# Centring x3 where it is scaled, group norm batch by batch, and the weights' product as a stage, in a four-block attention kernel

## The chip, the cores and the metric

One core of a Trainium2 chip runs the whole program. The metric is device time in microseconds (us), as a median of several executions; times within the kernel come from one profiled execution.

## The reference, cut to what matters

The input x is (2, 128, 16, 16) in fp32: two batches, 128 channels, 256 positions. Four blocks follow each other:

```python
# L0: group norm (32 groups of 4 channels), q, k, v, attention over 256 positions, projection, residual
xn = ((xr - mu) * rsqrt(var + 1e-6)) * gamma + beta
# L1: position attention (16-wide q and k) and channel attention, both added to x
# L2: attention with 8 heads of 16 channels on x and an embedding; output projection and residual: x3
# L3: f = (x3 - mean_c(x3)) * rsqrt(var_c(x3) + 1e-5) * norm_g
q = dwconv3x3(conv1x1(f, q_w), q_dw)          # the same for k and v
q = softmax(q, over d) * scale ; k = softmax(k, over n)
out = silu(q @ (k^T v)) ; out = chan_ln(conv1x1(out, out_w)) + x3
h = gelu(conv1x1(chan_ln(out), ff_w1)) ; result = conv1x1(chan_ln(h), ff_w2) + out
```

The change touches the group norm of L0 and the channel norm with which L3 begins.

## The kernel before, in words

Channels lie on the 128 partitions and the 256 positions on the free axis; some tiles are held with positions on partitions (names ending in T). There is no loop over tiles at run time: each engine has a list of stages, each with a batch number, written out by hand at the end of its section (GpSimd L272, ScalarE L489, VectorE L873, TensorE L1308). Engines run their lists in order and meet through semaphores, so the order of work is that of the four lists. All eight PSUM banks are shared out by hand, batch b mostly using banks 4b to 4b+3. The input and the weights come as seven transfers: x of batch 0, pack_a in two pieces, pack_b, pack_c and the taps from SyncE's queue, x of batch 1 from ScalarE's.

The start: TensorE multiplies a tile of zeros eight times (`keep_clock`, L910), then waits for the statistics of both batches. VectorE takes statistics (L539), aggregates them (L543), adds the squared mean (L547). One matmul with a group averaging matrix (L916) serves both batches; VectorE copies its result out of PSUM (L550), forms the negated square (L553) and the variance (L556); GpSimd raises it to the power -1/2 (L224); VectorE forms scale (L559) and shift (L563) and normalises x into hn0 (L568). TensorE does three more dummy products, the product of the weights wv0 and wpT0 (L920, L921), whose result VectorE evacuates to wpvT (L572), and two more dummies. Then come the stages: q (L926) and k (L930) of the normalised x, scores (L944), maxima (L589), exponentials (L298), v (L934), transposed probabilities (L973), the mix (L1001), and x1 as t times the row scale plus xb0 (L624, L627).

The L3 block folds the channel mean into the weights: GpSimd scales the 1x1 weights by norm_g into wg (L235), TensorE multiplies them by a matrix of 1/128 (`wg_mean`, L951), VectorE subtracts the result, giving wgc (`centre_wg`, L699), and GpSimd multiplies wgc by the nine taps of q into convw (L240). x3 with positions on partitions is summed in PSUM by an identity product (`x3_ident`, L1178) and the output projection (`x3_tokens`, L1185). VectorE takes its statistics (L526, L530, L533), GpSimd the inverse root (`root3`, L221), ScalarE scales each row (`f_scale`, L392) into fT, TensorE transposes it (`f_transposes`, L1192), ScalarE evacuates it (`f_evac`, L399) with two shifted copies (L402, L403). From f: q by nine products per half with convw (`conv`, L1213), k by one product (L1199) and nine VectorE steps (`k_taps`, L789 and L792), v by one product (L1222), nine ScalarE products per batch (`v_products`, L412) and eight GpSimd additions per batch (`v_sums`, L269). Behind them: transposes of v (L1228), the context product (L1241), the output products, the feed-forward part. `ff_mean_1` (L959) is a mean matmul of the feed-forward weights, between the transposes of v of batch 1 and its context product.

The group norm's middle, on VectorE and GpSimd, in the kernel's own words:

```python
nc.vector.scalar_tensor_tensor(ve0[:, :], gs0[:, :, 1], EPS_GN, nm0[:, :], ALU.add, ALU.add).then_inc(s["ve0_d"], 1)
nc.gpsimd.tensor_tensor(rstd0[:, :], ve0[:, :], mhalf[:, 0:NB], ALU.pow).then_inc(s["rstd0_d"], 1)
```

## Time and profile before

| | us |
|---|---|
| median of 3 runs | 83.71 |
| lowest and highest | 83.67, 83.97 |
| the profiled execution | 83.64 |
| its span in the profile | 81.8 |

Of the span, TensorE is busy for 71.5 us, VectorE 57.2, ScalarE 48.7, GpSimd 30.5. The weight loads of TensorE (PEld) overlap its matmuls; an fp32 matmul appears as two instructions, so counts on TensorE are twice the number in the code. Merged pieces such as "x4" are consecutive instructions of a line. "Idle before" in brackets is the time that the engine stood still before the piece, and what ended it, as far as the profile can infer it.

### The profile page before, as it was taken

What the parts mean: (1) busy time and instruction counts of PE and PEld (TensorE: products, weight loads), DVE (VectorE), ACT (ScalarE), POOL (GpSimd) and SP (SyncE); (2) the same over time, 40 slices, a digit from 0 to 9 for tenths busy, and PEclk for the clock granted to TensorE, in tenths of its full rate; (3) what the DMA queues carried; (4) which work ended last, traced back from release to release, by engine and by line L of the source; (5) the groups of instructions that cost most, each with busy time, mean ns of one, the idle gap of its engine ahead of it and who ended that gap; (6) DMA issues with size and microseconds to landing.
All of it is one profiled execution on the core that took longest, in us unless ns stands there. A gap on an engine that the chain in (4) does not pass through costs nothing.

```text
span 81.8 us, 1629 instructions
## 1 busy us (share of the span) xinstructions
PE 71.5 (87%) x563; PEld 53.7 (66%) x563; DVE 57.2 (70%) x210; ACT 48.7 (60%) x133; POOL 30.5 (37%) x62
## 2 busy tenths in 40 slices
PE   4978999999999997939898999999998579779960
PEld 1325799847888775737456656998997277646830
DVE  1357887897678649776688243699999838898540
ACT  4300487368843608395968398997998634627530
POOL 7913450005953364000000030488878712155400
PEclk9999999999999999999999999999999999999999
DMA  1999700000000000000000000000000000000003
GB/s 17 204 331 404 288 0 0 0 0 8 0 4 0 4 0 0 0 0 8 0 0 0 8 0 0 0 0 0 8 0 4 0 0 0 4 0 0 0 3 126
DMA packets 1304, 2.91 MB, mean 36 GB/s; under 512 B 144, under 2 KB 784, under 8 KB 1296
## 3 DMA queue, kind: packets, MB, share of 16 engines
q1 hardware_dynamic: 1152, 2.68, 9.8%
q10 hardware_dynamic: 144, 0.13, 0.5%
q8 instruction: 4, 0.07, 0.3%
q14 instruction: 4, 0.03, 0.1%
HBM read 2.55 MB, written 0.26 MB: 34 GB/s over the span
## 4 chain that ended last, share of the span: by engine, by line
PE 63%; DVE 17%; POOL 7%; ACT 4%; DMA 3%; issue 2%; POOLq 0%
PE bank L1213 9%; DVE nmx L748 6%; PE bank L1112 5%; PE bank L1151 4%; DMA x<-in_x 3%; POOL vacc L269 3%; POOL rs L221 3%; PE bank L1290 3%; PE bank L1138 2%; PE bank L1055 2%; PE bank L1001 2%; PE bank L973 2%; PE bank L944 2%; PE bank L1038 2%; PE bank L1124 2%
## 5 line engine op out<-in xcount | busy, mean ns | idle before, releaser
L221 POOL TENSOR_TENSOR rs<-ve,mhalf 128x2 f32<-128x2 f32 x8 | 5.6, 696 | 23.2 <-DVE ve L533 23.1
L269 POOL TENSOR_TENSOR vacc<-vacc,vprod 128x240 f32<-128x240 f32 (+1 forms) x16 | 10.8, 675 | 5.5 <-ACT vprod L412 3.8
L376 ACT ACTIVATE pT<-bank 128x512 f32<-128x512 f32 x16 | 8.5, 602 | 1.7 <-PE bank L1138 1.3
L1213 PE MATMUL bank<-convw,fsh 128*128 128x128 f32 x72 | 9.2, 275 | 0.0
L1213 PEld LDWEIGHTS bank<-convw,fsh 128*128 128x128 f32 x72 | 8.7, 193 | 0.1
L748 DVE TENSOR_REDUCE nmx<-bank 128x2 f32<-128x512 f32 x10 | 6.4, 687 | 3.2 <-PE bank L1112 3.2
L240 POOL TENSOR_TENSOR convw<-wgc,tapw 128x128 f32<-128x128 f32 x9 | 3.8, 453 | 8.0 <-DVE wgc L699 8.0
L412 ACT ACTIVATE vprod<-bank,wc 128x256 f32<-128x256 f32 x16 | 6.6, 492 | 0.0
L792 DVE SCALAR_TENSOR_TENSOR kacc<-bank,wc,kacc 128x240 f32<-128x240 f32 (+1 forms) x16 | 6.3, 447 | 0.0
L910 PE MATMUL bank<-warm 128*128 128x512 bf16 x13 | 4.8, 517 | 1.2 <-DVE warm L535 1.2
L1112 PE MATMUL bank<-km,qm 32*128 32x256 f32 x64 | 4.6, 400 | 0.0
L1151 PE MATMUL bank<-pT,v 128*32 128x256 f32 x64 | 4.3, 385 | 0.0
L1138 PE MATMUL bank<-qa,km 32*128 32x256 f32 x64 | 4.3, 381 | 0.0
L1124 PE MATMUL bank<-wa,nmx 128*128 128x128 f32 x8 | 1.7, 297 | 2.4 <-DVE nmx L742 1.7
L371 ACT ACTIVATE km<-bank,kone,kmask 128x256 f32<-128x256 f32 x4 | 2.0, 558 | 2.9 <-PE bank L1088 2.9
L476 ACT ACTIVATE excess<-bank 128x256 f32<-128x256 f32 x6 | 2.0, 380 | 2.8 <-PE bank L1112 2.8
L288 ACT ACTIVATE k<-bank,wa 128x256 f32<-128x256 f32 x2 | 0.9, 476 | 4.5 <-PE bank L930 4.5
L1112 PEld LDWEIGHTS bank<-km,qm 32*128 32x128 f32 x64 | 2.9, 184 | 0.9 <-issue 0.5
L910 PEld LDWEIGHTS bank<-warm 128*128 128x128 bf16 x13 | 1.5, 137 | 2.9 <-issue 1.7
L1138 PEld LDWEIGHTS bank<-qa,km 32*128 32x128 f32 x64 | 3.1, 185 | 0.4 <-DVE qa L756 0.2
L1124 PEld LDWEIGHTS bank<-wa,nmx 128*128 128x128 f32 x8 | 0.8, 140 | 3.7 <-DVE nmx L742 2.6
L526 DVE BATCH_NORM_STATS2 st<-bank 128x6 f32<-128x128 f32 x8 | 2.0, 290 | 1.6 <-PE bank L1185 1.6
(215 smaller groups left out, 186.9 us busy)
## 6 DMA issues: line engine op xcount, KB each, us to landing
wc<-in_pack_c SPq DMA_DIRECT2D x1, 649.0 KB, 6.7
wb<-in_pack_b SPq DMA_DIRECT2D x1, 612.0 KB, 5.6
tapw<-in_taps SPq DMA_DIRECT2D x1, 576.0 KB, 7.6
wa<-in_pack_a SPq DMA_DIRECT2D x1, 320.0 KB, 4.5
out<-y SPq DMA_DIRECT2D x2, 128.0 KB, 1.7
x<-in_x ACTq DMA_DIRECT2D x1, 128.0 KB, 2.8
x<-in_x SPq DMA_DIRECT2D x1, 128.0 KB, 2.7
wa<-in_pack_a SPq DMA_DIRECT2D x1, 72.5 KB, 2.6
```

The lines of the kernel that those rows point to most:

```text
L221: nc.gpsimd.tensor_tensor(dst, src, mhalf[:, 0:width], ALU.pow).then_inc(done, 1)
L269: nc.gpsimd.tensor_add(vacc[b][:, oy, ox], vacc[b][:, oy, ox], vprod[n - 1][b][:, iy, ix]).then_inc(s[f"vsum_d{b}"], 1)
L376: nc.scalar.activation(pT2[u % PT2_RING][:, :, :], tiles(bank[SCORE_T_BANKS[u % HG]]), ACT.Exp).then_inc(s["e2_d"], 1)
L412: nc.scalar.activation(dst, LC[b][:, 0:N].rearrange("p (h w) -> p h w", h=H), ACT.Copy, scale=tap("vdw", *CENTRE_FIRST[n])).then_inc(s[f"v ...
L748: nc.vector.tensor_reduce(nmx2[g][:, :, col:col + 1], tiles(bank[SCORE_BANKS[i]]), AX.X, ALU.max, negate=True).then_inc(s["max2_d"], 1)
L792: nc.vector.scalar_tensor_tensor(acc, k1x1[:, iy, ix], tap("kdw", dy, dx), acc, ALU.mult, ALU.add).then_inc(s["vec"], 1)
L910: nc.tensor.matmul(dst[:, :], warm[:, 0:128], warm[:, :], start=True, stop=True)
L1112: product = nc.tensor.matmul(tiles(bank[SCORE_BANKS[i]])[:, t, :], qm2[b][rows, g, t * 128:(t + 1) * 128], keys, start=True, stop=True, ti ...
L1124: last = nc.tensor.transpose(bank[SHIFT_BANK[grp]][:, t * 128:(t + 1) * 128], nmx2[grp % NG][:, t, :], ident)
L1138: product = nc.tensor.matmul(tiles(bank[SCORE_T_BANKS[i]])[:, t, :], km2[b][rows, g, t * 128:(t + 1) * 128], qa2[b][rows, g, :], start=Tru ...
L1151: last = nc.tensor.matmul(bank[MIX_BANK[grp]][QUAD * i:QUAD * (i + 1), 0:N], v2[b][:, kt, g * C + QUAD * i:g * C + QUAD * (i + 1)], pT2[(g ...
L1213: product = nc.tensor.matmul(LA[b][:, j * C:(j + 1) * C], fsh[dx][b][:, row:row + H // NT, :].rearrange("p h w -> p (h w)"), convw[:, 3 * ...
```

## The change

x3 is now centred where it is scaled: VectorE forms minus mean times inverse root (`x3_shift`, mrs3), and ScalarE's scaling takes it as a bias. The mean matmul of the 1x1 weights and its subtraction are gone, and wg stands where wgc stood. The group norm runs batch by batch: one small mean matmul for each into bank 4b, the square by ScalarE, variance by VectorE from PSUM, one root for each batch. The product of wv0 and wpT0 becomes a stage of TensorE's list (`wpv_products`, bank 6), its evacuation the first stage of VectorE's. Seven dummy products instead of eight open the program, and the last two are gone. The stage lists of all engines are in a new order, among it: both v products of L0 together, `half_masks` early, `v_product` of L1 for batch 1 where the mean matmul was, `f_transposes` of batch 0 behind the mixed transposes of batch 1, `ff_mean_1` ahead of the second batch's transposes, `root3` of batch 1 after one sum instead of three. Waits that the new order needs are added.

```diff
-pool.wait_ge(s["ve0_d"], 1)
-nc.gpsimd.tensor_tensor(rstd0[:, :], ve0[:, :], mhalf[:, 0:NB], ALU.pow).then_inc(s["rstd0_d"], 1)
+for b in range(NB):
+    pool.wait_ge(s["ve0_d"], b + 1)
+    nc.gpsimd.tensor_tensor(rstd0[:, b:b + 1], ve0[:, b:b + 1], mhalf[:, 0:1], ALU.pow).then_inc(s["rstd0_d"], 1)
...
-pool.wait_ge(s["wgc_w"], 1)
+pool.wait_ge(s["prep_w"], PREP_WG)
 pool.wait_ge(s["tap_in"], 16)
 for t in range(TAPS):
-    nc.gpsimd.tensor_tensor(convw[:, t, :], wgc[:, C:2 * C], tapw[:, t * C:(t + 1) * C], ALU.mult).then_inc(s["conv_w"], 1)
+    nc.gpsimd.tensor_tensor(convw[:, t, :], wg[:, C:2 * C], tapw[:, t * C:(t + 1) * C], ALU.mult).then_inc(s["conv_w"], 1)
...
+for stage, b in ((xb2_sum, 0), (key_steps, 0), (xb2_sum, 1), (key_steps, 1), (root3, 0), (v_sums(1, 2), 0), (root3, 1),
+    (v_sums(2, TAPS), 0), (v_sums(1, TAPS), 1), (root4, 0), (root4, 1), (root5, 0), (root5, 1), (root6, 0),
...
+for b in range(NB):
+    act.wait_ge(s["g0_p"], b + 1)
+    nc.scalar.activation(gsq0[:, b:b + 1], bank[4 * b][:, 0:1], ACT.Square).then_inc(s["gsq_d"], 1)
...
-    act.wait_ge(s["rs3_d"], b + 1)
-    for t in range(NT):
-        nc.scalar.activation(fT[b][:, t, :], tiles(LA[b], 4)[:, t, :], ACT.Copy, scale=rs3[b][:, 0, t:t + 1]).then_inc(s["fT_d"], 1)
+    act.wait_ge(s["mrs3_d"], b + 1)
+    for t in range(NT):
+        nc.scalar.activation(fT[b][:, t, :], tiles(LA[b], 4)[:, t, :], ACT.Identity, bias=mrs3[b][:, t:t + 1],
+                             scale=rs3[b][:, 0, t:t + 1]).then_inc(s["fT_d"], 1)
...
+    (head_excess(1, 2), 1), (head_excess(1, 3), 1), (head_exps(0, 0, 3), 1), (mixed_evac_of(1), 0),
+    (head_exps(0, 3, 4), 1), (head_exps(1, 0, 4), 1), (mixed_evac_of(0), 1), (x3T_evac, 0),
+    (mixed_evac_of(1), 1), (f_scale, 0), (f_evac, 0), (o2_evac, 1), (v_products(0, 2), 0), (shift_edges, 0),
+    (v_products(2, 7), 0), (f_scale, 1), (v_products(7, TAPS), 0), (x3T_evac, 1), (f_evac, 1), (shift_edges, 1),
+    (k_exp, 0), (v_products(0, 2), 1), (q_exp, 0), (v_products(2, 8), 1), (ekT_evac, 0),
+    (v_products(8, TAPS), 1), (v3_evac, 0), (qT_evac, 0), (k_exp, 1), (q_exp, 1), (ekT_evac, 1), (o3_tanh, 0),
...
-for b in range(NB):
+def group_inputs(b):
     dve.wait_ge(s[f"x{b}_in"], 16)
     nc.vector.bn_stats(st0[b][:, :], x0[b][:, :]).then_inc(s["vec"], 1)
     vec_done("st0")
-for b in range(NB):
-    dve.wait_ge(s["vec"], vec_at("st0", b + 1))
+    dve.wait_ge(s["vec"], vec_last("st0"))
     nc.vector.bn_aggr(mv0[:, b, :], st0[b][:, :]).then_inc(s["vec"], 1)
     vec_done("mv0")
-for b in range(NB):
-    dve.wait_ge(s["vec"], vec_at("mv0", b + 1))
+    dve.wait_ge(s["vec"], vec_last("mv0"))
     nc.vector.scalar_tensor_tensor(mv0[:, b, 1:2], mv0[:, b, 0:1], mv0[:, b, 0:1], mv0[:, b, 1:2],
                                    ALU.mult, ALU.add).then_inc(s["gin0_d"], 1)
-dve.wait_ge(s["g0_p"], 1)
-nc.vector.tensor_copy(gs0[:, :, :].rearrange("p b m -> p (b m)"), bank[0][:, 0:2 * NB]).then_inc(s["vec"], 1)
...
+
+def group_variance(b):
+    dve.wait_ge(s["gsq_d"], b + 1)
+    nc.vector.tensor_scalar(ve0[:, b:b + 1], bank[4 * b][:, 1:2], EPS_GN, gsq0[:, b:b + 1],
+                            ALU.add, ALU.subtract).then_inc(s["ve0_d"], 1)
+    nc.vector.tensor_scalar_mul(gm0[:, b:b + 1], bank[4 * b][:, 0:1], A("gamma")).then_inc(s["vec"], 1)
+    vec_done("gm0")
+
+def group_norm(b):
+    dve.wait_ge(s["rstd0_d"], b + 1)
+    nc.vector.tensor_scalar_mul(a0[:, b:b + 1], rstd0[:, b:b + 1], A("gamma")).then_inc(s["vec"], 1)
+    vec_done("a0")
+    dve.wait_ge(s["vec"], vec_at("gm0", b + 1))
+    nc.vector.tensor_scalar(nb0[:, b:b + 1], gm0[:, b:b + 1], rstd0[:, b:b + 1], A("beta"),
+                            ALU.mult, ALU.subtract).then_inc(s["vec"], 1)
     vec_done("nb0")
-for b in range(NB):
     dve.wait_ge(s["vec"], vec_at("nb0", b + 1))
     nc.vector.tensor_scalar(hn0[b][:, :], x0[b][:, :], a0[:, b:b + 1], nb0[:, b:b + 1],
                             ALU.mult, ALU.subtract).then_inc(s["hn0_d"], 1)
 
+for stage, b in ((group_inputs, 0), (group_inputs, 1), (group_variance, 0), (group_variance, 1),
+    (group_norm, 0), (group_norm, 1)):
+    stage(b)
+
+def wpvT_evac(b):
+    dve.wait_ge(s["wpv_p"], 1)
+    nc.vector.tensor_copy(wpvT[:, :], bank[6][:, 0:C]).then_inc(s["wpv_w"], 1)
+    nc.vector.tensor_add(bias0[:, :], bank[6][:, C:C + 1], A("bp0")).then_inc(s["wpv_w"], 1)
...
-def centre_wg(b):
-
-    dve.wait_ge(s["wgm_p"], 1)
-    nc.vector.tensor_sub(wgc[:, :], wg[:, :], bank[7][:, 0:3 * C]).then_inc(s["wgc_w"], 1)
...
+def x3_shift(b):
+    dve.wait_ge(s["rs3_d"], b + 1)
+    nc.vector.scalar_tensor_tensor(mrs3[b][:, :], mv3[b][:, 0, :, 0], -1.0, rs3[b][:, 0, :], ALU.mult, ALU.mult).then_inc(s["mrs3_d"], 1)
...
+for stage, b in ((wpvT_evac, 0), (xb0_sum, 0), (q0_evac, 0), (q0_evac, 1), (xb0_sum, 1), (max0(0), 0), (max0(1), 0),
+    (max0(0), 1), (max0(1), 1), (sums0, 0), (half_masks, 0), (p0T_evac(0), 0), (p0T_evac(0), 1), (sums0, 1),
+    (centre_outw, 0), (x1_sum, 0), (x1_sum, 1), (q1_evac, 0), (xb1_sum, 0), (xb1_sum, 1), (q1_evac, 1),
+    (max1(0), 0), (max1(1), 0), (max1(0), 1), (p1T_evac(0), 0), (max1(1), 1), (sums1, 0), (pam_sum(0), 0),
+    (pam_sum(1), 0), (sums1, 1), (p1T_evac(0), 1), (energy_min, 0), (pam_sum(0), 1), (pam_sum(1), 1),
+    (ce_scale, 0), (ceT_evac, 0), (energy_min, 1), (outw_scale, 0), (x2_sum, 0), (ce_scale, 1), (ceT_evac, 1),
     (q2_evac, 0), (x2_sum, 1), (head_maxes(0, 0, 4), 0), (q2_evac, 1), (shift_add_of(0), 0),
     (head_maxes(1, 0, 4), 0), (shift_add_of(1), 0), (head_maxes(0, 0, 4), 1), (shift_add_of(0), 1),
+    (head_maxes(1, 0, 4), 1), (o2_norm_of(0), 0), (shift_add_of(1), 1), (o2_norm_of(1), 0), (o2_evac, 0),
+    (x3_stats, 0), (x3_shift, 0), (o2_norm_of(0), 1), (o2_norm_of(1), 1), (x3_stats, 1), (k_taps(0, 3), 0),
+    (x3_shift, 1), (k_taps(3, TAPS), 0), (k_max, 0), (q_max, 0), (k_taps(0, 6), 1), (q_norm, 0),
+    (k_taps(6, TAPS), 1), (k_max, 1), (q_max, 1), (k_sums, 0), (context, 0), (q_norm, 1), (centre_ff_1, 0),
+    (silu, 0), (k_sums, 1), (context, 1), (y_stats, 0), (silu, 1), (x4_sum, 0), (y_stats, 1), (x4_stats, 0),
+    (x4_sum, 1), (centre_ff_2, 0), (x4_stats, 1), (h_stats, 0), (h_stats, 1), (y_sum, 0), (y_sum, 1)):
...
-keep_clock(8, bank[7])
-pe.wait_ge(s["gin0_d"], NB)
-pe.wait_ge(s["a_in"], 16)
-nc.tensor.matmul(bank[0][:, 0:2 * NB], A("gmean"), mv0[:, :, :].rearrange("p b m -> p (b m)"),
-                 start=True, stop=True).then_inc(s["g0_p"], 1)
+keep_clock(7, bank[7])
+for b in range(NB):
+    pe.wait_ge(s["gin0_d"], b + 1)
+    if b == 0:
+        pe.wait_ge(s["a_in"], 16)
+    nc.tensor.matmul(bank[4 * b][:, 0:2], A("gmean"), mv0[:, b, :], start=True, stop=True).then_inc(s["g0_p"], 1)
 keep_clock(3, bank[7])
-pe.wait_ge(s["a2_in"], 16)
-nc.tensor.matmul(bank[3][:, 0:C], A("wv0"), A("wpT0"), start=True, stop=True)
-nc.tensor.matmul(bank[3][:, C:C + 1], A("wpT0"), A("bv0"), start=True, stop=True).then_inc(s["wpv_p"], 1)
-keep_clock(2, bank[7])
+def wpv_products(b):
+    pe.wait_ge(s["a2_in"], 16)
+    nc.tensor.matmul(bank[6][:, 0:C], A("wv0"), A("wpT0"), start=True, stop=True)
+    nc.tensor.matmul(bank[6][:, C:C + 1], A("wpT0"), A("bv0"), start=True, stop=True).then_inc(s["wpv_p"], 1)
...
-def wg_mean(b):
-
-    pe.wait_ge(s["prep_w"], PREP_WG)
-    nc.tensor.matmul(bank[7][:, 0:3 * C], K("cmean"), wg[:, :], start=True, stop=True).then_inc(s["wgm_p"], 1)
...
-    nc.tensor.matmul(LC[b][:, 0:N], wgc[:, 2 * C:3 * C], fsh[1][b][:, 1:H + 1, :].rearrange("p h w -> p (h w)"),
+    nc.tensor.matmul(LC[b][:, 0:N], wg[:, 2 * C:3 * C], fsh[1][b][:, 1:H + 1, :].rearrange("p h w -> p (h w)"),
...
+for stage, b in ((wpv_products, 0), (k0_product, 0), (q0_product, 0), (q0_product, 1), (k0_product, 1), (scores0(0), 0),
+    (scores0(1), 0), (scores0(0), 1), (scores0(1), 1), (v0_product, 0), (v0_product, 1), (p0_transposes(0), 0),
+    (scale0, 0), (p0_transposes(0), 1), (p0_transposes(1), 0), (p0_transposes(1), 1), (mix0(0), 0), (scale0, 1),
+    (mix0(1), 0), (mix0(0), 1), (mix0(1), 1), (qk1_product, 0), (v1_product, 0), (qk1_product, 1), (scores1, 0),
+    (xb1_transposes, 0), (v1_product, 1), (scores1, 1), (xb1_transposes, 1), (p1_transposes(0), 0),
+    (p1_transposes(1), 0), (mix1(0), 0), (mix1(1), 0), (p1_transposes(0), 1), (p1_transposes(1), 1),
+    (energy, 0), (mix1(0), 1), (mix1(1), 1), (pam_transposes, 0), (ce_transpose, 0), (embedding(1), 0),
+    (energy, 1), (outw_transpose, 0), (co_product, 0), (embedding(0), 0), (pam_transposes, 1),
+    (ce_transpose, 1), (qk2, 0), (co_product, 1), (outwg_transpose, 0), (embedding(0), 1), (embedding(1), 1),
+    (of_group(group_scores, 0), 0), (v2_product, 0), (qk2, 1), (v2_product, 1),
     (of_group(max_transposes, 0), 0), (of_group(group_scores, 1), 0), (of_group(group_scores_T, 0), 0),
     (of_group(max_transposes, 1), 0), (of_group(group_scores, 0), 1), (of_group(group_scores_T, 1), 0),
     (of_group(group_mix, 0), 0), (of_group(max_transposes, 0), 1), (of_group(group_scores, 1), 1),
     (of_group(group_scores_T, 0), 1), (of_group(group_mix, 1), 0), (mixed_transposes_of(0), 0),
+    (of_group(max_transposes, 1), 1), (mixed_transposes_of(1), 0), (of_group(group_scores_T, 1), 1),
+    (o2_transposes, 0), (x3_ident, 0), (x3_tokens, 0), (of_group(group_mix, 0), 1), (of_group(group_mix, 1), 1),
+    (mixed_transposes_of(0), 1), (x3_ident, 1), (mixed_transposes_of(1), 1), (f_transposes, 0),
+    (o2_transposes, 1), (v_1x1, 0), (x3_tokens, 1), (k_1x1, 0), (conv(0, 0, TAPS), 0), (conv(1, 0, 3), 0),
+    (f_transposes, 1), (conv(1, 3, TAPS), 0), (k_1x1, 1), (v_1x1, 1), (conv(0, 0, 6), 1), (v_transposes, 0),
+    (ek_transposes, 0), (conv(0, 6, TAPS), 1), (conv(1, 0, 6), 1), (q_transposes, 0), (conv(1, 6, TAPS), 1),
+    (ctx_product, 0), (ff_mean_1, 0), (ek_transposes, 1), (o3_product, 0), (v_transposes, 1), (q_transposes, 1),
+    (ctx_product, 1), (y_products, 0), (o3_product, 1), (ff_mean_2, 0), (yg_products, 0), (y_products, 1),
+    (x4_transposes, 0), (yg_products, 1), (h_products, 0), (x4_transposes, 1), (h_products, 1),
+    (h_transposes, 0), (h_transposes, 1), (ff_product, 0), (ff_product, 1), (y_transposes, 0), (y_transposes, 1)):
```

## Rows read from the trace of the kernel before

**Rows 1.** The page, its parts 1 and 2: busy time of each engine, granted clock of TensorE.
```profile
PE 71.5 (87%) x563; PEld 53.7 (66%) x563; DVE 57.2 (70%) x210; ACT 48.7 (60%) x133; POOL 30.5 (37%) x62
...
PEclk9999999999999999999999999999999999999999
```

**Rows 2.** Chain of waits, whole span: start us, us, what held it.
```profile
5.83 0.71 POOL rstd L224
...
7.55 0.70 PE bank L926 x2
...
9.54 1.77 PE bank L944 x8
...
15.33 0.56 PE bank L1010 x2
...
18.01 0.65 PE bank L951 x2
...
21.99 0.71 PE bank L1068 x4
...
50.57 0.60 PE bank L1222 x2
...
65.20 0.64 POOL vacc L269
...
65.88 0.44 PE bank L1228 x2
66.32 0.43 PE bank L959 x2
```

**Rows 3.** Timeline of DVE, 0 to 11: start us, us, instruction, count [idle before].
```profile
3.42 0.75 DVE L539 BATCH_NORM_STATS2 st<-x 128x6 f32<-128x256 f32 x2 [2.30 <-DMA x<-in_x]
4.09 0.30 DVE L543 BATCH_NORM_AGGREGATE mv<-st 128x2 f32<-128x6 f32 x2
...
7.09 0.73 DVE L568 TENSOR_SCALAR hn<-x,a,nb 128x256 f32<-128x256 f32 x2
...
8.29 0.48 DVE L576 TENSOR_SCALAR q<-bank,wa 128x256 f32<-128x256 f32 x1 [0.21 <-PE bank L926]
...
9.58 0.48 DVE L576 TENSOR_SCALAR q<-bank,wa 128x256 f32<-128x256 f32 x1 [0.29 <-PE bank L926]
10.01 1.33 DVE L589 TENSOR_REDUCE nmax<-bank 128x1 f32<-128x256 f32 x3
```

**Rows 4.** Timeline of PE, 0 to 11.
```profile
1.17 3.38 PE L910 MATMUL bank<-warm 128*128 128x512 bf16 x8 [1.17 <-DVE warm L535]
...
4.94 0.81 PE L910 MATMUL bank<-warm 128*128 128x512 bf16 x3
6.19 0.49 PE L920 MATMUL bank<-wa 128*128 128x128 f32 x2 [0.43 <-DMA wa<-in_pack_a]
```

**Rows 5.** Timeline of ACT, 0 to 11.
```profile
3.76 0.43 ACT L284 ACTIVATE bqk<-wa 32x2 f32<-32x2 f32 x2 [1.33 <-DMA wa<-in_pack_a]
```

**Rows 6.** Timeline of DVE, 11 to 29.
```profile
14.72 0.42 DVE L627 TENSOR_TENSOR x<-t,xb 128x256 f32<-128x256 f32 x1
...
18.70 0.56 DVE L699 TENSOR_TENSOR wgc<-wg,bank 128x384 f32<-128x384 f32 x1 [0.23 <-PE bank L951]
```

**Rows 7.** Timeline of POOL, 0 to 29.
```profile
10.75 0.58 POOL L235 TENSOR_SCALAR wg<-wc,wa 128x384 f32<-128x384 f32 x1
19.34 3.76 POOL L240 TENSOR_TENSOR convw<-wgc,tapw 128x128 f32<-128x128 f32 x9 [8.00 <-DVE wgc L699]
```

**Rows 8.** Timeline of POOL, 44 to 69.
```profile
52.12 2.34 POOL L269 TENSOR_TENSOR vacc<-vacc,vprod 128x240 f32<-128x240 f32 x3 [3.32 <-ACT vprod L412]
...
61.19 4.64 POOL L269 TENSOR_TENSOR vacc<-vacc,vprod 128x240 f32<-128x240 f32 x6 [0.46 <-ACT vprod L412]
```

**Rows 9.** Timeline of ACT, 44 to 69.
```profile
59.33 1.57 ACT L412 ACTIVATE vprod<-bank,wc 128x256 f32<-128x256 f32 x4
```

**Rows 10.** Timeline of DVE, 60.7 to 61.3.
```profile
60.89 0.42 DVE L816 TENSOR_TENSOR qn<-eq,rq 128x256 f32<-128x256 f32 x1
```

More of the change, by code:

```diff
@@ L76, in build @@
         convw = sb("convw", [128, TAPS, C])
-        wg, wgc = sb("wg", [128, 3 * C]), sb("wgc", [128, 3 * C])
+        wg = sb("wg", [128, 3 * C])
         wpvT = sb("wpvT", [128, C])
@@ L97, in build @@
         mv0 = sb("mv0", [128, NB, 2])
-        gs0 = sb("gs0", [128, NB, 2])
-        nm0, ve0, rstd0, a0, nb0 = (sb(name, [128, NB]) for name in ("nm0", "ve0", "rstd0", "a0", "nb0"))
+        gsq0, gm0, ve0, rstd0, a0, nb0 = (sb(name, [128, NB]) for name in ("gsq0", "gm0", "ve0", "rstd0", "a0", "nb0"))
         hn0 = per_batch("hn0", [128, N])
@@ L283, in _ @@
             for t in range(NT):
-                nc.scalar.activation(bqk[QUAD * t:QUAD * (t + 1), :], wa[0:QUAD, at_a["bq1"][0]:at_a["bk1"][1]], ACT.Copy).then_inc(s["bqk_w"], 1)
+                nc.scalar.activation(bqk[QUAD * t:QUAD * (t + 1), :], wa[0:QUAD, at_a["bq1"][0]:at_a["bk1"][1]], ACT.Copy)
+            for b in range(NB):
+                act.wait_ge(s["g0_p"], b + 1)
+                nc.scalar.activation(gsq0[:, b:b + 1], bank[4 * b][:, 0:1], ACT.Square).then_inc(s["gsq_d"], 1)
             def k0_evac(b):
@@ L565, in _ @@
+            def group_norm(b):
[5 more added lines that the diff above has]
+                                        ALU.mult, ALU.subtract).then_inc(s["vec"], 1)
                 vec_done("nb0")
-            for b in range(NB):
@@ L932, in v0_product @@
             def v0_product(b):
+                if b == 0:
+                    pe.wait_ge(s["wpv_w"], 1)
                 for t in range(NT):
@@ L1060, in pam_transposes @@
             def pam_transposes(b):
+                pe.wait_ge(s[f"pamT_d{NT - 1}"], b + 1)
                 for t in range(NT):
@@ L1090, in v2_product @@
             def v2_product(b):
+                pe.wait_ge((s["q2_d"], s["k2_d"])[b], NG)
                 for t in range(NT):
@@ L1176, in x3_ident @@
                     pe.wait_ge(s["e2_d"], 3 * HG + 2)
+                pe.wait_ge(s["xb2_d"], b + 1)
                 for t in range(NT):
@@ L1198, in k_1x1 @@
                 pe.wait_ge(s["f_d"], b + 1)
-                nc.tensor.matmul(LD[b][:, 0:N], wgc[:, 0:C], fsh[1][b][:, 1:H + 1, :].rearrange("p h w -> p (h w)"),
+                nc.tensor.matmul(LD[b][:, 0:N], wg[:, 0:C], fsh[1][b][:, 1:H + 1, :].rearrange("p h w -> p (h w)"),
                                  start=True, stop=True).then_inc(s["k1x1_p"], 1)
```

75 lines of the change are left out of this document (8 added, 67 removed).

## Prediction

> **What bounds the kernel now.** I read the page first: TensorE is busy for 87% of the span, no other engine for more than 70%, and the granted clock is at its top in every slice [rows 1]. So most of the span is a queue of matmuls, and work taken off the other engines is worth nothing where that queue is full. Next the chain of waits, for the places where it leaves TensorE [rows 2]. There are three that this change touches. The group norm: VectorE, one matmul and GpSimd's power alternate until the first product starts at 7.55. The middle, from the query product at 15.33 to the group scores, where the chain lies on TensorE alone, so that a matmul there costs its full length. And the depthwise sums of v: GpSimd's additions for the second batch end at 65.84, and only then come the transposes at 65.88. Last, the timelines, for what can be packed closer.
>
> Profiled execution and runs: the sum is made against the profiled execution's own 83.64 us (span 81.8), 0.07 below the median of 83.71. A difference of under 0.5%, 0.42 us, can't be told from none.
>
> **Term A, group norm per batch.** Before, statistics, aggregates and squares of both batches are ready by about 4.65 and one root serves both. Now VectorE finishes batch 0 alone: half of the 0.75 of statistics, one aggregate (some 0.15) and one square (some 0.17) with 0.04 between dependent steps bring it from 3.42 to about 4.2, and batch 1 to about 5.0 [rows 3]. That part loses 0.35, since each batch waits out its own dependent steps. The mean matmul (0.4) and the new square on ScalarE, which no row shows, fit under batch 1's statistics: a tiny activation took about 0.22 (two in 0.43) [rows 5], so batch 0's is done at about 4.85. Its bounds are 0.2 and 0.5; at the upper end the variance is 0.1 late. What goes is the copy out of PSUM and the negated square. The variance of batch 0 starts at 5.02, and the root, a tiny step and a handshake of 0.16 later, at 5.34 where it starts at 5.83 now; it takes 0.71 for two columns [rows 2]; for one column I take the same (bounds 0.5 and 0.71, the row being of the same operation). It ends at 6.05, not 6.54. Then scale, shift (one, not two) and normalisation: the normalised x begins at 6.51, and the first product at 6.9 against 7.55. Batch 1's root queues behind the first: 6.15 to 6.85, its normalised x from 7.27 to 7.62, where it ended at 7.82 [rows 3].
>
> The weights' product needs the second piece of pack_a, for which TensorE waited until 6.19 [rows 4]; it runs 6.19 to about 6.8 and hides. Its evacuation (some 0.35) and one addition of xb0 (some 0.3) now stand on VectorE before q's evacuation. That costs: q0 of batch 0 is evacuated at 8.3, no earlier than now at 8.29 [rows 3]. Yet k and q of both batches are all out of TensorE at 6.9 + 4 x 0.43 = 8.6, not at 9.54, so the scores start at 8.78 instead of 9.54 [rows 2]: 0.76. VectorE has 10.01 - 7.82 = 2.19 between normalised x and the first maximum, 0.50 of it waits for TensorE (0.21 and 0.29) [rows 3]; without them the maxima start at 7.62 + 1.69 = 9.3 at the earliest, 9.4 with the handshakes: 0.6. From there the same 4.0 us of matmuls leads to the query product, now at 15.33 [rows 2]. The half masks now stand inside this stretch (about 0.4 on VectorE, before a transposed probability tile that TensorE wants at 12.55 and gets at 12.2), so they are covered. **A = 0.70**, between 0.6 and 0.76.
>
> **Term B, no centring of the 1x1 weights.** It takes away a matmul of 0.65 on the chain at 18.01 [rows 2] and VectorE's subtraction of 0.56 at 18.70 [rows 6]. The v product of batch 1, about 0.44, moves into the same place, so the scores behind it gain only 0.2 at once. VectorE reaches the next maximum 0.6 earlier, and the first mix waits for its evacuated tile, then for nothing: following maxima, exponentials and evacuations one by one, TensorE is idle about 0.25, and the energy product at 21.99 [rows 2] comes at 20.8, that is 1.2 earlier including A. **B = 0.50**; bounds 0.2 (only the immediate gain) and 0.65 (the whole matmul). From there to 44 the order of a few stages changes; TensorE stays full to the group scores, then VectorE's maxima set the pace as now: I count nothing.
>
> GpSimd's nine tap products (3.76) waited until 19.34 for the centred weights; now they wait only for the scaled ones, ready at 11.33 [rows 7]. Nobody needs them before the convolution, which stands behind the v product at 50.57, so the gain is nothing; what they may collide with is below.
>
> **Term C, x3 centred where it is scaled.** Per batch VectorE gets one tiny product (some 0.17 like the other tiny ones, plus two hops of 0.04), and ScalarE's scaling takes a bias too, at most 0.05 more per tile. On batch 0 it is hidden: in the new order ScalarE takes the second mixed tile of batch 1 ahead of the scaling, and by my walk is busy with it until 0.4 after the shift. If that cover were gone it would cost 0.25. ScalarE now does three exponentials ahead of the mixed tile instead of one, which frees the transposed scores by about 0.6; but TensorE then takes transposes ahead of x3's. Walking all four engines through this stretch with the durations of before, the v product, now at 50.57 and 0.60 long [rows 2], ends at 51.3 against 51.17. GpSimd's sums, which start behind it at 52.12 [rows 8], start at 52.2; the second batch's root, now after one sum, waits about 0.1 for its variance. **C = -0.15**, bounds +0.3 and -0.7. From 52.12 to 65.84 these sums and the root, 16 and 1, are the bound.
>
> **Term D, behind the sums.** The feed-forward mean matmul, 0.43 between the transposes of v and the context product [rows 2], moves into TensorE's idle time. ScalarE's evacuation of v still takes 0.4 after the transposes, so 0.2 is left of it: **D = 0.20**, bounds 0 and 0.43. The x4 transposes go ahead of a product but the second batch sets the end.
>
> Sum: 0.70 + 0.50 - 0.15 + 0.20 = 1.25.
>
> **A collision, term E.** GpSimd's addition at 61.19 came 0.46 after the one before [rows 8], though its tile, the first of the four written from 59.33 on, had been ready for over a microsecond [rows 9]; just then VectorE ran a product of two SBUF operands, 60.89 to 61.23 [rows 10]. So such pairs can exclude each other. In the new order the tap products, 11.4 to 15.2, lie over VectorE's addition of t and xb0, two SBUF operands, 0.42 [rows 6], on the path at about 14.1 and again at 15.0. Each may wait for a running tap product of 0.42: from nothing to 0.42 on the first, little on the second, which has 0.15 of slack. I take 0.15. The Trainium skill (SBUF — State Buffer, "Who interferes with whom") says VectorE and GpSimd share one port pair as an exclusive lock, for two SBUF inputs and also for VectorE's fast scaling in SBUF. By that rule, the trace at 61.19 agrees; the normalised x, at 6.51, would also stand behind the second root. What it gives is a rival below.
>
> Forecast: 83.64 - 1.25 + 0.15 = 82.54, and 0.07 for the median: **82.6**. Its own range is 82.2 to 83.0.
>
> **Rivals.**
> (1) The lock in full, 0.16. Normalised x of batch 0 waits for the root of batch 1, 6.51 to 6.85, 0.35 that VectorE passes on to everything behind it, and the addition waits 0.42 more. For: the 0.46 at 61.19. Against: small VectorE steps ran beside GpSimd's roots unhindered in the tail. Result 83.64 - 1.25 + 0.77 = 83.2, with the median 83.2 to 83.3.
> (2) The order loses the gain in the conv part, 0.17: C at its bound or a little past it, since x3's scaling stands behind another evacuation on ScalarE and v's sums start 0.7 later. For: the start of the sums hangs there on a chain through all four engines, each in a new order. Against: the walk finds other work for TensorE at every point but two, 0.2 each. Result 83.64 - 1.10 + 0.6 = 83.1 to 83.5.
> (3) Slower, 0.07: TensorE's clock. The first eight dummy matmuls took 0.42 each, the three from 4.94 on 0.27 with their latency [rows 4]: same shape, so the clock went from 1.2 to 2.4 GHz at about 4.5. The change issues seven, and leaves TensorE with a tiny matmul only between 4.1 and 5.05. If the clock were still low when k's product starts, the 3.5 us of products and scores from 6.9 to 10.5 would take up to 7.0: 82.5 + 3.5 = 86.0. It decides at 6.9: rising by then it costs nothing, at 8.6 it costs 1.7, that is 84.3. Against: the granted clock is full in every slice [rows 1], and one dummy of eight is little.
> That the square could need a table of its own is the remaining mishap; it would show as a second table load before 5.
>
> **Chances.** Forecast 0.60, lock 0.16, order 0.17, clock 0.07. Faster by over 0.5% (below 83.29): nearly all of the first, three quarters of the second, half of the third: 0.58 + 0.12 + 0.08 = 0.78. Slower (above 84.13): the clock and a tail of the order: 0.08. Same: 0.14. The range 81.9 to 83.5 takes in A, B and D at their upper bounds (0.4 more) with no collision, and both middle rivals, and leaves out the clock and the tails.
>
> **What would show it.** Right: first product on hn at about 6.9, query product at 14.6, energy at 20.8, v's sums starting 1.1 to 1.2 earlier (about 51.0), transposes of v at 64.7, no wgc. Tap products right behind wg. Wrong: normalised x starting only when the second root ends; an addition at 14 that begins late; dummy products of 0.42 past 5; sums that start less than 0.8 earlier, which would put the loss in term C; or a GpSimd chain that got longer between its ends.

## The result and the profile after

The changed kernel is slower: 85.16 us as the median of four runs, against 83.76 for four runs of the kernel before beside them, a ratio of 1.0159 (95% interval 1.0133 to 1.0186). The prediction was 82.6, at most 83.5. The profiled execution took 85.18 with a span of 83.4; the one before took 83.64 with 81.8. The difference of these two, 1.54, is what is traced below. Executions of one and the same kernel fall into two groups here, around 83.8 and around 85.1, and a ratio compares the lower group where a kernel has one; the four of the changed kernel have none (85.06, 85.14, 85.18, and 86.77), the four beside them have only that.

The stages, from the chains of waits of four executions (us from the span's start; the last two columns are experiments that come below):

| start of | before | after | eighth dummy back (e1) | dense, late taps (f3) |
|---|---|---|---|---|
| scores, L0 | 9.54 | 10.56 | 9.13 | 8.85 |
| query product, L1 | 15.33 | 16.60 | 15.08 | 14.78 |
| energy product | 21.99 | 22.96 | 21.58 | 21.37 |
| first transposed maxima, L2 | 32.29 | 33.25 | 31.87 | 31.50 |
| last transposed scores, L2 | 45.27 | 45.53 | 44.15 | 43.79 |
| x3 with positions on partitions, batch 0 | 46.34 | 47.56 | 46.18 | 45.82 |
| v product, batch 0 | 50.57 | 52.24 | 50.85 | 50.50 |
| transposes of v, batch 1 | 65.88 | 67.45 | 66.06 | 65.69 |

Two things stand in it. The changed kernel is 1.02 behind before its first scores. And from the last transposed scores to the v product it loses 1.41 more, having gained 0.76 up to there.

**The page**, parts 1 and 2. Where [rows 1] stood, nothing looks wrong:

```profile
PE 73.1 (88%) x560; PEld 55.1 (66%) x560; DVE 58.3 (70%) x213; ACT 49.2 (59%) x135; POOL 31.3 (38%) x63
...
PEclk9999999999999999999999999999999999999999
```

TensorE has three instructions fewer and is busy for 1.6 us more. The same work took longer. The timeline of TensorE, 0 to 12, says where:

```profile
1.17 3.17 PE L915 MATMUL bank<-warm 128*128 128x512 bf16 x7 [1.17 <-DVE warm L540]
4.44 0.59 PE L923 MATMUL bank<-mv,wa 128*128 128x2 f32 x2
5.25 0.59 PE L923 MATMUL bank<-mv,wa 128*128 128x2 f32 x2 [0.22 <-DVE mv L550]
5.69 1.44 PE L915 MATMUL bank<-warm 128*128 128x512 bf16 x3
...
7.64 1.20 PE L936 MATMUL bank<-hn,wa 128*128 128x256 f32 x2
8.63 1.49 PE L932 MATMUL bank<-hn,wa 128*128 128x256 f32 x4
9.96 0.59 PE L936 MATMUL bank<-hn,wa 128*128 128x256 f32 x2
```

Three dummies take 1.44 where they took 0.81 [rows 4], and the first product 1.20 where it took 0.70 [rows 2]. Those are durations of the lower level, 1.2 GHz; k of batch 1, at 9.96, is the first piece wholly at the upper one, 2.4 GHz. Before, the level had risen by the dummies at 4.94. The row of the granted clock is all nines in both kernels, so it doesn't tell of this opening; the duration of a known shape does.

**VectorE, 4 to 18:**

```profile
6.08 0.22 DVE L555 TENSOR_SCALAR ve<-bank,gsq 128x1 f32<-128x1 f32 x1 [0.46 <-ACT gsq L288]
...
6.76 0.41 DVE L569 TENSOR_SCALAR hn<-x,a,nb 128x256 f32<-128x256 f32 x1
...
15.29 0.78 DVE L691 TENSOR_SCALAR outwc<-outwc,outws 128x128 f32<-128x128 f32 x1
15.49 0.57 DVE L631 TENSOR_TENSOR t<-bank,rb 128x256 f32<-128x256 f32 x1
16.12 0.42 DVE L634 TENSOR_TENSOR x<-t,xb 128x256 f32<-128x256 f32 x1
```

The variance of batch 1 stands in VectorE's list ahead of the scale of batch 0 and waits for ScalarE's square. The scaling of outwc at 15.29 takes 0.78, beside the last of GpSimd's tap products (11.71 to 15.49) and the clearing of a tile behind them (to 15.99); with the tap products moved away (f3) it takes 0.29. It also takes 0.29 in e1, where they run as here, so what is held up changes with where the steps fall. The sum x of t and xb comes late behind it, and the query product at 16.60 waits 0.28 for it.

**The chain of waits**, whole span, to set against [rows 2]:

```profile
10.56 1.77 PE bank L952 x8
...
32.09 1.03 ACT km L375 x2
...
45.53 1.15 PE bank L1141 x16
46.68 0.38 PE bank L1173 x2
47.06 0.02 issue
47.08 0.44 DVE o L774
47.52 0.04 issue
47.56 0.71 PE bank L1189 x4
48.27 1.86 PE bank L1154 x32
50.14 0.37 PE bank L1166 x2
50.51 0.45 PE bank L1182 x4
50.95 0.23 PE bank L1166 x2
...
51.80 0.44 PE bank L1173 x2
52.24 0.60 PE bank L1226 x2
...
66.62 0.79 POOL vacc L269
67.40 0.04 issue
67.45 0.45 PE bank L1232 x2
67.92 0.39 ACT v L437
68.31 0.04 issue
68.36 0.71 PE bank L1245 x4
```

The transposed scores of the last group run ahead of three pieces that ran before them in the old order: the transposes of o2 (L1173), VectorE's copy of them, and x3's identity product. Then come the 32 matmuls of the mix and the second mix's transposes. From 51.18 to 51.80 TensorE has only the transposes of f to do and waits for VectorE, before the last transposes of o2, which now stand ahead of the v product. That is 2.03 to x3 and 4.68 on to the v product, where it was 1.07 and 4.23. A second chain ends nearly as late there: ScalarE's scaling of x3 and the evacuation of f, which the v product reads, end at 52.08 (the line at 51.70 below).

**Shift and scaling of x3**, both batches, VectorE and then ScalarE, 47 to 60:

```profile
50.14 0.16 DVE L781 SCALAR_TENSOR_TENSOR mrs<-mv,rs 128x2 f32<-128x2 f32 x1 [0.84 <-POOL rs L220]
...
55.56 0.41 DVE L781 SCALAR_TENSOR_TENSOR mrs<-mv,rs 128x2 f32<-128x2 f32 x1
```

```profile
50.49 0.80 ACT L396 ACTIVATE fT<-bank,mrs,rs 128x128 f32<-128x128 f32 x2
51.70 0.39 ACT L404 ACTIVATE fsh<-bank 128x256 f32<-128x256 f32 x1 [0.42 <-PE bank L1196]
...
56.00 0.81 ACT L396 ACTIVATE fT<-bank,mrs,rs 128x128 f32<-128x128 f32 x2
```

The shift (mrs) takes 0.16 with GpSimd quiet and 0.41 while GpSimd adds products of v. Scaling with a bias takes 0.80 for two tiles; without one it took 0.62 (g4 below).

### The profile page after: what moved, and what is told of

The parts are those of the page before. It is cut to its first block, busy times and chain, and to the rows that moved or that the text cites. A ratio compares the mean times of both kernels' runs of the same rounds, so it can differ in the third digit from the quotient of the medians.

```text
span 83.4 us, 1630 instructions
## 1 busy us (share of the span) xinstructions
PE 73.1 (88%) x560; PEld 55.1 (66%) x560; DVE 58.3 (70%) x213; ACT 49.2 (59%) x135; POOL 31.3 (38%) x63
## 4 chain that ended last, share of the span: by engine, by line
PE 57%; DVE 16%; ACT 11%; POOL 7%; DMA 3%; issue 3%; POOLq 0%
PE bank L1115 5%; PE bank L1217 5%; POOL vacc L269 4%; ACT vprod L417 4%; DMA x<-in_x 3%; DVE nmx L750 3%; POOL rs L220 3%; PE bank L1294 2%; ACT pT L380 2%; PE bank L1056 2%; PE bank L1141 2%; PE bank L1154 2%; PE bank L1090 2%; PE bank L952 2%; PE bank L1039 2%
## 5 line engine op out<-in xcount | busy, mean ns | idle before, releaser
L246 POOL TENSOR_SCALAR xb<-x,wa 128x256 f32<-128x256 f32 x2 | 2.3, 1147 | 11.0 <-DVE x L722 11.0
L240 POOL TENSOR_TENSOR convw<-wg,tapw 128x128 f32<-128x128 f32 x9 | 3.8, 457 | 0.1
```

Of the source, the lines that this page charges most:

```text
L240: nc.gpsimd.tensor_tensor(convw[:, t, :], wg[:, C:2 * C], tapw[:, t * C:(t + 1) * C], ALU.mult).then_inc(s["conv_w"], 1)
```

## Experiments

Theory T: the clock of the opening makes the time, because seven dummies stand where eight stood. Rivals: the added waits and orders, the two engines' collision, the centring itself.

**e1, the eighth dummy back, and nothing else.**

```diff
-            keep_clock(7, bank[7])
+            keep_clock(8, bank[7])
```

> The changed kernel with eight opening dummy products instead of seven. Clock theory: the array was still at the low level up to 9.6 in the changed kernel because TensorE did too little before 4.6; with the eighth the products of k and q run at the high level, the scores start at about 9.0 to 9.2 and not 10.56, and the time is 83.6 to 83.9, 1.3 to 1.5 below the changed kernel. Rival (the gap between the two mean matmuls keeps the clock low, whatever the eighth does): scores at 10.5, time 85.1.

Ten executions: five at 83.72 to 83.86, five at 85.05 to 85.74; ratio of the lower group 0.9997 (0.9978 to 1.0016). The profiled one took 83.79. TensorE, 0 to 11:

```profile
5.57 0.81 PE L915 MATMUL bank<-warm 128*128 128x512 bf16 x3
...
7.13 0.70 PE L936 MATMUL bank<-hn,wa 128*128 128x256 f32 x2 [0.42 <-DVE hn L569]
```

Every stage of the table is 1.38 to 1.52 earlier than in the changed kernel: a rise of the clock ahead of the first products instead of at about 9.6 is worth 1.4. It makes up all but 0.15 of the difference of 1.54.

That the eighth dummy brings the early rise is not shown. Five of ten executions with it are still in the upper group, and against four of four without it that can be chance (probability 0.13 if both had one rate). What is shown is that this loss belongs to the changed opening. The mean granted clock tells the two losses apart: with the late rise it reads 1.00 (the changed kernel's profile), with a fall at 66 it reads 0.98 (e2 below). All 32 upper executions of the kernel before with its eight dummies, of 81 in three series, read 0.975 to 0.980. Of the 28 of the changed kernel, e1, e3 and e4 together, 14 are in the upper group with 1.00.

**e2, the kernel before with seven dummies.** The same edit on the other side (8 to 7).

> The kernel before with seven opening dummy products instead of eight, nothing else. Clock theory with the count as its cause: the clock stays low here too, the scores start 1 to 2 late and the time is 84.8 to 85.8. Rival (the spread of the small products is the cause): unchanged, 83.7.

All four executions at 85.09 to 85.14, ratio 1.0157 (1.0137 to 1.0177), next to the changed kernel's 1.0159. Its start, however, is at the upper level: the three dummies at 4.99 take 0.81. The clock falls late; page, then TensorE's timeline, 60 to 74:

```profile
PEclk9999999999999999999999999999999858999999
```

```profile
65.92 0.69 PE L1228 MATMUL bank<-wa,vacc 128*128 128x128 f32 x2 [1.16 <-POOL vacc L269]
66.40 1.06 PE L959 MATMUL bank<-w1g,wc 128*128 128x256 f32 x2
...
67.68 1.06 PE L1241 MATMUL bank<-v,ekT 128*128 128x128 f32 x4
```

L959 takes 1.06 where it took 0.60, behind an idle wait of 1.16 for GpSimd's last sum that the kernel before has too. So there are two places where the level can be lost, the opening and the wait at 65, and either costs 1.3 to 1.5. The mean clock of this execution is 0.977. Two of the changed kernel's own runs show 0.976 (85.06) and 0.98 (86.77), so it loses in either place, the second perhaps in both. What ties the number of dummies to a fall at 66 no run shows: the kernel before falls there with eight as well, in 32 of 81 executions. At that rate four of four in the upper group would be chance once in 40, so seven may make it likelier. One of the four (85.09) reads 1.00 and was not profiled; it may have lost at the opening.

**e3, a dummy between the two mean matmuls of the changed kernel** (seven opening ones kept), and **e4, eight dummies and the tap products held back until x1 is summed:**

```diff
 nc.tensor.matmul(bank[4 * b][:, 0:2], A("gmean"), mv0[:, b, :], ...)
+if b == 0:
+    keep_clock(1, bank[7])
```
```diff
 pool.wait_ge(s["tap_in"], 16)
+pool.wait_ge(s["x1_d"], NB)
```

> The changed kernel with one dummy product between the two mean matmuls, seven ahead as it has them. If the idle time between 4.1 and 5.25 is what holds the clock down, this brings the scores to 9.0 to 9.3 and the time to 83.7 to 84.0; if only what TensorE did before about 4.5 counts, the scores stay at 10.5 and the time at 85.1 or a little above, since the dummy delays the second mean by up to 0.2.

> Eight opening dummies as in the first run, and GpSimd's tap products wait until both x1 are there (about 15.5) instead of starting right behind the scaled weights. Lock theory: VectorE's scalings and its addition into x1 no longer meet them, the query product comes 0.2 earlier than in the first run, and the time is 0.1 to 0.25 lower (the opposite risk: they now meet VectorE's work from 16 to 20). Rival: no difference, within 0.1.

e3: five of ten at 83.58 to 83.93, five at 84.86 to 85.87; with the gap filled or with a dummy ahead, half of the executions lose. e4: one of four at 83.55, the rest at 84.90 to 85.35, and in its profile, eight dummies or not, the three behind the mean matmuls take 1.44. Its time says nothing of the taps. Its profile, with a late rise as in the changed kernel's, has 5.79 from the scores to the query product against 6.04, but 12.38 against 12.40 to the energy product: the tap products then meet VectorE's next work. Nothing of the size of a few tenths can be read while the clock is left to chance, so the next kernels fill both places.

**f1, the kernel before with its late waits filled:** two dummies ahead of the transposes of k's exponentials of batch 1, four ahead of those of v of batch 1.

```diff
+def fill(n):
+    return lambda b: keep_clock(n, bank[4])
-(ctx_product, 0), (ek_transposes, 1), (o3_product, 0), (v_transposes, 1)
+(ctx_product, 0), (fill(2), 1), (ek_transposes, 1), (o3_product, 0), (fill(4), 1), (v_transposes, 1)
```

> The kernel before with six dummy products in TensorE's idle time behind the context product of batch 0 (two, then four, ahead of the transposes of v of batch 1). Theory: the executions at 84.9 to 85.1 that the kernel before also has lose their time to the clock, which falls once in that idle stretch (between 63 and 66) and is low for some 3 us; with TensorE kept busy there, that loss goes and executions lie at 83.6 to 84.0, but for those where the clock rises late at the start. Rival (the falls come from elsewhere): the two levels remain as often as in the kernel before, which has 7 of 19 at the upper one.

All ten executions at 83.41 to 83.92, median 83.77, ratio 1.000 (0.998 to 1.002), while 11 of the 31 unfilled ones beside them took 84.91 or more. The other versions of the kernel before with this filling (g1, g2, g4) don't fall into two groups either. TensorE, 60 to 70: the wait of 1.16 is down to 0.29, and L959 takes its 0.60.

```profile
64.86 1.03 PE L910 MATMUL bank<-warm 128*128 128x512 bf16 x4
66.19 0.44 PE L1231 MATMUL bank<-wa,vacc 128*128 128x128 f32 x2 [0.29 <-POOL vacc L269]
66.47 0.60 PE L959 MATMUL bank<-w1g,wc 128*128 128x256 f32 x2
```

**f2, the changed kernel made dense:** e1 and e3 together, one dummy behind the weights' product, and four ahead of the transposes of v of batch 1. **f3** is f2 with e4's wait; **f4** is f2 with the stage lists of all engines, from 43 to 53, in the order of before:

```diff
-(mixed_evac_of(0), 1), (x3T_evac, 0), (mixed_evac_of(1), 1), (f_scale, 0), (f_evac, 0), (o2_evac, 1)
+(mixed_evac_of(0), 1), (f_scale, 0), (mixed_evac_of(1), 1), (f_evac, 0), (x3T_evac, 0), (shift_edges, 0)
...
-(root3, 0), (v_sums(1, 2), 0), (root3, 1), (v_sums(2, TAPS), 0)
+(root3, 0), (v_sums(1, 4), 0), (root3, 1), (v_sums(4, TAPS), 0)
```

> The changed kernel with eight opening dummies, one between the two mean matmuls, one behind the weights' product, and four in the idle time ahead of the transposes of v of batch 1. Theory: what the change costs is the clock alone and, with that mended, its orders give 83.7 to 83.9, no better than the kernel before. The profile should show the high level before 8 and no fall later; the upper level (85) should be gone or rare. Rival (dummies don't help the start): still 85 in half of the executions.

> As the filled changed kernel, with GpSimd's tap products held until both x1 are written. Lock theory: the additions into x1 and the scalings take their usual 0.20 to 0.43 instead of up to 0.57, the query product comes 0.1 to 0.2 earlier against the filled changed kernel, and the time is 0.1 to 0.2 lower, unless the tap products meet other steps of VectorE later. Rival: within 0.1.

> As the filled changed kernel, with the stage order between the last transposed scores and the convolution (TensorE, ScalarE, VectorE, and the second root of GpSimd) put back to that of the kernel before; centring by the bias stays. Theory that the new order there costs 0.7: the v product comes 0.6 to 0.8 earlier and the time is 83.1 to 83.3 against 83.8. Rival (centring by a bias costs the 0.7 itself, through the extra step and the longer scaling): it stays within 0.2 of the filled changed kernel.

| kernel | median of 10 | lowest to highest | ratio (95%) |
|---|---|---|---|
| f1, before, filled | 83.77 | 83.41 to 83.92 | 1.000 (0.998 to 1.002) |
| f2, after, dense | 83.94 | 83.70 to 84.24 | 1.0027 (1.0004 to 1.0049) |
| f3, f2 with late taps | 83.63 | 83.42 to 83.95 | 0.9967 (0.993 to 1.0005) |
| f4, f2 with the old order | 84.99 | 84.68 to 85.45 | 1.0154 (1.0128 to 1.018) |

None of these four kernels falls into two groups. f2 against the changed kernel: 1.2, the clock's; which of its dummies does it is not separated. f2 against f1: with the clock held, the change is worth 0.17 in the wrong direction, which is no difference by the measure of 0.42. f3 against f2: 0.31, though its profile shows only 0.11 of it between the scores and the query product (5.93 against 6.04 from one to the other), and that is lost again by the energy product (12.52 against 12.40 from the scores); its x also arrived 0.08 earlier. Where the 0.31 lie stays open. Its VectorE, 11 to 18, with nothing held up until the tap products start at 15.80; then xb takes 0.98 where it took 0.62:

```profile
13.46 0.29 DVE L692 TENSOR_SCALAR outwc<-outwc,outws 128x128 f32<-128x128 f32 x1
13.85 0.42 DVE L632 TENSOR_TENSOR t<-bank,rb 128x256 f32<-128x256 f32 x1
14.30 0.42 DVE L635 TENSOR_TENSOR x<-t,xb 128x256 f32<-128x256 f32 x1
...
16.30 0.98 DVE L648 TENSOR_SCALAR xb<-x,gbv 128x256 f32<-128x256 f32 x2
```

f4 says that the new order, blamed above for 1.41 on the way to the v product, is a repair: without it the centring costs 1.05 more. The v product of batch 0 was expected 0.6 to 0.8 earlier and comes at 50.62 against 50.67 in f2: with the order of the exponentials put back as well, the last transposed scores start at 45.18 against 44.05. And batch 1 pays. VectorE and ScalarE of f4, 53 to 59:

```profile
55.47 0.56 DVE L781 SCALAR_TENSOR_TENSOR mrs<-mv,rs 128x2 f32<-128x2 f32 x1
```

```profile
56.06 0.81 ACT L396 ACTIVATE fT<-bank,mrs,rs 128x128 f32<-128x128 f32 x2 [1.77 <-DVE mrs L781]
```

The root now stands behind three sums, the shift behind the root and beside a fourth sum, and ScalarE stands still for 1.77 in front of its scaling, with the products of v for GpSimd queued behind it.

**g1, the centring alone, in the kernel before** (filled as f1): wg for wgc, no mean matmul, shift and bias as in the change, everything else and its order as before, the taps held back to x1. **g4** is g1 without shift and bias: it leaves out the centring of x3. **g2** is f1 with the group norm per batch alone, and e3's dummy. **g3** is f3 with x3 centred and scaled by VectorE in one step for each tile instead of the shift and ScalarE's scaling:

```diff
-nc.vector.scalar_tensor_tensor(mrs3[b][:, :], mv3[b][:, 0, :, 0], -1.0, rs3[b][:, 0, :], ALU.mult, ALU.mult)
+for t in range(NT):
+    nc.vector.tensor_scalar(fT[b][:, t, :], tiles(LA[b], 4)[:, t, :], mv3[b][:, 0, t, 0:1], rs3[b][:, 0, t:t + 1], ALU.subtract, ALU.mult)
```

> The kernel before with the filled idle time, and of the change only x3 centred by the bias (no mean matmul, no subtraction, one shift step per batch, tap products behind x1); group norm and all orders as before. Theory: the mean matmul gives back 0.4, but the shift and the longer scaling lengthen the chain from x3 to the v product by 0.45 for batch 0 and, behind root and tap steps, more for batch 1, so the time is 83.8 to 84.6 against 83.78 of the filled kernel before. Rival (the bias is free, as forecast): 83.2 to 83.4.

> As the centring-only kernel but with no shift either: x3's mean is not subtracted at all, so this leaves out the centring of the channel norm (the output is not the reference's). Only the mean matmul and its subtraction are gone against the filled kernel before. Theory: 83.2 to 83.5, 0.3 to 0.5 below it; the difference to the centring-only kernel, 0.5 to 1.2, is what the bias costs. Rival (removing the matmul gains nothing): 83.8.

> The kernel before with the filled idle time and of the change only the group norm batch by batch (two mean matmuls with a dummy between, square on ScalarE, two roots); orders as before. Theory: the first product starts 0.35 to 0.45 earlier, not 0.65, and the time is 83.3 to 83.5 if nothing gives it back. Rival (the later stages don't follow): 83.7 to 83.8.

> The filled changed kernel with late tap products, but x3 is centred and scaled by VectorE in one instruction per tile (x minus mean, times root), instead of a shift on VectorE and a scaling with bias on ScalarE; ScalarE's copy of x3 is ahead of it, for batch 1 moved up. Theory: the chain from the root to f's transposes of batch 0 shortens from 1.2 to about 0.65, GpSimd's sums start 0.4 to 0.5 earlier and the time is 83.1 to 83.3 against 83.63: the first version clearly below the kernel before. Rival (VectorE, busy in this stage, gives it back on batch 1): 83.5 to 83.8.

| kernel | median of 10 | lowest to highest | ratio (95%) |
|---|---|---|---|
| g1, centring where it is scaled | 84.74 | 84.52 to 84.99 | 1.0081 (1.0046 to 1.0115) |
| g4, no centring at all | 83.81 | 83.55 to 83.94 | 0.9974 (0.9945 to 1.0003) |
| g2, group norm per batch | 83.42 | 83.36 to 84.10 | 0.9947 (0.9901 to 0.9993) |
| g3, centring on VectorE | 83.99 | 83.86 to 84.23 | 0.9998 (0.9959 to 1.0036) |

These four were timed on another chip than f1 to f4; the lower group of the kernel before has its median at 83.89 beside them and at 83.78 beside the f kernels. So a difference of a g kernel from an f kernel is good to 0.1 or 0.2, and those among the g kernels are better.

g4 against f1: the matmul of 0.65 and the subtraction of 0.56, gone without anything in their place, show no gain (83.81 against 83.77; by the ratios 0.2). g4's profile takes 12.46 from the scores to the energy product, as before (12.45). The place is taken by another wait; TensorE, 16 to 23:

```profile
17.99 0.44 PE L1031 MATMUL bank<-wa,xb 128*128 128x128 f32 x2 [0.29 <-DVE xb L641]
```

VectorE's xb, two steps of 0.98 together beside the tap products, is what the chain now goes through. But they take 0.98 only because the tap products, held back to x1, start at 16.45 in g4; in the kernel before they take 0.62. So g4 shows that this version gains nothing, and not that the matmul was free: a version without it and with the tap products behind xb was not run.

g1 against g4: 0.93 is the price of the shift and the bias in the old order. In g1's profiled execution the clock rose late, the three dummies behind the mean matmul taking 1.44 where they take 0.81 in g4 and in the kernel before, all with the same opening; the first products come after the rise there, and it costs 0.2:

```profile
5.21 1.44 PE L916 MATMUL bank<-warm 128*128 128x512 bf16 x3
```

ScalarE of g1 and then of g4, 53 to 59:

```profile
56.36 0.81 ACT L393 ACTIVATE fT<-bank,mrs,rs 128x128 f32<-128x128 f32 x2 [0.62 <-DVE mrs L781]
```

```profile
55.34 0.62 ACT L393 ACTIVATE fT<-bank,rs 128x128 f32<-128x128 f32 x2
```

The start is 1.02 later, 0.43 of which the v product of batch 0 already shows (50.93 against 50.50; 0.19 lie ahead of the first scores), and the scaling is 0.19 longer. The transposes of v of batch 1 come 1.11 later (67.06 against 65.95). g2 is the only part that gains: 0.35 against f1, or 0.5% by its ratio, the lowest of the study, with an interval that overlaps f3's. g3 doesn't beat f3: from x3 to the v product it takes 4.68, like the changed kernel. Its f is evacuated 0.28 sooner after x3 than e1's (3.87 against 4.15), but the v product stands behind the last transposes of o2 in TensorE's list, and those wait for VectorE; on batch 1 VectorE gives back another 0.5 (15.69 against f3's 15.19 from the v product to the transposes of v). TensorE of g3, 49 to 54:

```profile
50.31 0.44 PE L1180 MATMUL bank<-wa,onT 128*128 128x128 f32 x2 [0.41 <-DVE onT L769]
```

## Why the prediction was wrong

The profiled execution lies 2.64 above the 82.54 of the sum. Two steps failed, of about the same size: the clock was put at nothing, and it cost 1.39; and the terms were to give 1.10 net and gave -0.15, which is 1.25.

**Rival (3), the clock, is what happened, and it had 0.07.** The step that failed is its last sentence, "the granted clock is full in every slice [rows 1], and one dummy of eight is little". The first half reads a row that is full in both kernels; the second weighs the dummy by its length, 0.42, and leaves out the rest of what the opening became. What was right is the mechanism: dummies of 0.42 past 5 were named as its sign. Its price was too high: 1.7 for a rise at 8.6, where the rise at about 9.6 cost 1.39. What the views of before held and the text passed over: the level had risen hardly ahead of 4.94 [rows 4], so that there was little to spare, and the change also opened a gap in front of the second mean matmul, named in the text and then not priced. How far the rise can move with nothing changed shows in executions that share the opening of before: ahead of 4.94 there, and past 6 in g1, still before the first product. The change brought the first products forward to 7.13 and thinned the work ahead of them. Whether the dummy, the gap or the missing last two decide stays open; the version with dummies at all three places (f2) loses in none of ten. The other edge, the fall at 66, could not be read from three runs either; it took 32 of 81 later executions of the kernel before.

**Term A, 0.70 forecast, 0.4 to 0.5 found.** With the clock mended (e1) the first product starts at 7.13 against the forecast 6.9, the scores at 9.13 against 8.78 (9.54 before), and x arrived 0.08 later in that execution: 0.49. The forecast let batch 0's scale follow its root at once; in VectorE's list the variance of batch 1 stands between, waiting for the square. The root itself started late, 5.65 against 5.34, and was shorter than taken, 0.55 against 0.71. From the first product to the scores it takes 2.00, as before (1.99), where the forecast had 1.88. At the query product 0.25 are left; VectorE, which has more to do in this stretch, and the collision take the rest. g2 gives 0.35 in the whole time. So the term had the right sign and about half the size.

**Term B, 0.50 forecast, 0.16 found between the query and the energy product** (e1: 6.50 against 6.66), and nothing from the scores to the energy product (12.45 in both). Its immediate part came: the scores of batch 1 follow the query product by 3.16 instead of 3.33. Its second part did not: the mix (L1056) waits for VectorE's copy of the transposed probabilities, and TensorE, with the v product gone from that place, stands idle for 0.30 ahead of it. In g4, with the old order and group norm, the whole term shows no gain, with the tap products in the way.

**Term C, -0.15 forecast.** The bound of -0.7 was nearer. From the last transposed scores to the v product the change loses 1.40 (e1: 6.70 against 5.30), having gained 0.70 with the three exponentials ahead of the mix (a gain that the text put at 0.6): -0.7 in all. The step that failed is the walk through this stretch; it found gaps of 0.2 at two points, and the trace has VectorE's copy in the chain (0.44) and another wait of 0.6 for the second batch's o2. This was rival (2) in its mechanism. The order makes it up in part for batch 1: the v product to the end of the sums takes 0.10 less than before, and without the order the whole kernel takes 1.05 more (f4). A second chain, the scaling of x3 and the evacuation of f, ends at 52.08, only 0.16 ahead of the v product, so shortening it alone gives nothing (g3). The tiny product was priced at 0.17; beside GpSimd's sums it takes 0.40 to 0.56. The bias was priced at 0.05 a tile and takes 0.09.

**Term D, 0.20 forecast, nothing found.** From the transposes of v to the statistics of y it takes 2.11 in both kernels (65.88 to 67.99, 67.45 to 69.56). The evacuation of v was said to take 0.4 of the 0.43 and 0.22 that lay over it; with its handshakes it takes 0.45, and the context product behind a wait takes 0.71, not 0.53.

**Term E and rival (1), the collision, -0.15 forecast, -0.1 to -0.25 found at the query product** (f3 against f2 0.11, e4 against the changed kernel 0.25), and nothing left of it at the energy product, since the tap products only met other steps when they were moved. The place was right (t and x at 15 to 16.5 in the changed kernel). The victim is the forecast's in e1 and f2, where x takes 0.57 and 0.54 instead of 0.42; in the changed kernel it is another, the scaling of outwc just ahead, with a single SBUF tensor. The Trainium skill (SBUF — State Buffer, "Who interferes with whom") says that VectorE's fast scaling in SBUF takes the port pair that it shares with GpSimd as an exclusive lock. By that rule, 0.78 against 0.29 agrees, and so does 0.98 against 0.62 for xb in f3 and g4; the 0.29 beside the tap products in e1 and f2 shows that such a step can also pass. The normalised x was not held back by the second root, as the rival in full had it: hn comes at 6.76 with that root running from 6.37 to 6.93.

By stages, e1's profile against the one before: 0.41 gained at the scores, then -0.16 to the query product, 0.16 to the energy product, 0.01 to the maxima, 0.70 to the last transposed scores, -1.40 to the v product, 0.10 to the end of the sums and 0.03 behind them, -0.15 in all. The clock takes 1.39 more.
